# Second quantised layer of a decoder: three filling steps moved into the cross attention before it, and its first bias added by TensorE

## The reference

```
def act_quant_fake(x):
    scale = 127.0 / clip(max(abs(x), -1), 1e-05)
    return clip(round(x * scale), -128.0, 127.0) / scale
def weight_quant_fake(w):
    scale = 1.0 / clip(mean(abs(w)), 1e-05)
    return clip(round(w * scale), -1.0, 1.0) / scale
def bitlinear(x, w, b):
    return einsum('btd,hd->bth', act_quant_fake(x), weight_quant_fake(w)) + b
h = layernorm(x, ln1_g, ln1_b)           # over 128 features
h = bitlinear(h, w1, b1)                 # 128 -> 512
h = gelu(h)                              # exact
h = layernorm(h, ln2_g, ln2_b)           # over 512
h = bitlinear(h, w2, b2)                 # 512 -> 128
x = layernorm(x + h)
```

## Time and profile before

| what | us |
|---|---|
| median of 3 runs (lowest, highest) | 1842.26 (1840.89, 1844.54) |
| the profiled execution | 1842.72 |
| its span, first to last instruction | 1840.9 |
| TensorE matmuls busy | 1510.0 (82%) |
| VectorE busy | 1110.9 (60%) |
| ScalarE busy | 874.4 (47%) |
| GpSimd busy | 610.7 (33%) |
| mean granted TensorE clock, share of full speed | 0.868 |

### The profile page before, as it was taken

One profiled execution on the slowest core, in us unless ns is written; L12 is line 12 of the kernel. 1 busy time (PEld: TensorE's weight loads), 2 busy tenths in 40 slices (PEclk: granted clock), 3 DMA queues, 4 the chain that ended last, 5 costly groups with the idle time before them and its releaser, 6 DMA issues.

```text
span 1840.9 us, 44133 instructions
## 1 busy us (share of the span) xinstructions
PE 1510.0 (82%) x16485; PEld 1018.2 (55%) x16492; DVE 1110.9 (60%) x3614; ACT 874.4 (47%) x2556; POOL 610.7 (33%) x849
## 2 busy tenths in 40 slices
PE   4556369979989769898889633699799999998998
PEld 3334246646656555455557412577577777776443
DVE  3434556656757557115767688577566666664776
ACT  3222335545556335443546544344366666665443
POOL 2422232222226333001212233222244444443666
PEclk6555569989999789999999855699899999999999
DMA  6200000000000000000020000000000000000000
GB/s 239 48 1 2 1 1 3 2 1 2 2 2 2 1 0 1 1 1 2 2 119 2 24 1 0 1 3 3 24 1 1 0 0 0 0 0 1 1 12 12
DMA packets 13994, 23.96 MB, mean 13 GB/s; under 512 B 11385, under 2 KB 11769, under 8 KB 12537
## 3 DMA queue, kind: packets, MB, share of 16 engines
q1 hardware_dynamic: 13818, 21.59, 3.3%
HBM read 18.15 MB, written 1.05 MB: 10 GB/s over the span
## 4 chain that ended last, share of the span: by engine, by line
PE 66%; DVE 12%; issue 7%; ACT 6%; POOL 4%; DVEq 3%; POOLq 1%; DMA 0%; ACTq 0%; another core or an unknown queue 0%; SPq 0%
PE ps L732 5%; PE ps L653 5%; PE ps L692 5%; PE ps L2884 4%; PE ps L2533 4%; PE ps L2543 3%; PE ps L2557 3%; PE ps L2512 3%; PE ps L2519 3%; PE ps L2356 2%; PE ps L613 2%; PE ps L1315 2%; PE ps L742 2%; PE ps L2504 2%; PE ps L719 2%
## 5 line engine op out<-in xcount | busy, mean ns | idle before, releaser
L919 DVE TENSOR_REDUCE arena<-ps 128x4 f32<-128x512 f32 x320 | 204.1, 683 | 111.9 <-PE ps L653 31.4
L857 ACT ACTIVATE arena<-ps 128x512 f32<-128x512 f32 x320 | 171.7, 597 | 99.2 <-PE ps L719 96.8
L544 POOL TENSOR_TENSOR arena<-arena,C 128x512 f32<-128x512 f32 x80 | 83.1, 1040 | 392.8 <-ACT arena L878 127.5
L2449 POOL TENSOR_TENSOR arena<-arena 128x512 f32<-128x512 f32 x128 | 132.7, 1042 | 224.4 <-DVE arena L2758 223.9
L1315 PE MATMUL ps<-hid,WA 128*20 128x16 f32 x1024 | 57.0, 196 | 88.2 <-DVE hid L1368 88.2
L2676 ACT COPY arena<-ps 128x512 f32<-128x512 f32 x128 | 69.1, 588 | 123.1 <-PE ps L2543 123.1
L2667 ACT ACTIVATE arena<-ps,arena 128x256 f32<-128x256 f32 x256 | 119.9, 477 | 11.8 <-issue 8.1
L2884 PE MATMUL ps<-WA,maskadd 128*128 128x512 f32 x256 | 119.8, 598 | 1.8 <-DVE arena L3027 1.8
L732 PE MATMUL ps<-arena 128*32 128x128 f32 x2560 | 110.8, 282 | 3.2 <-ACT arena L857 3.0
L653 PE MATMUL ps<-arena 32*128 32x128 f32 x2560 | 103.9, 288 | 10.0 <-POOL arena L544 7.0
L2750 DVE TENSOR_REDUCE arena<-ps 128x2 f32<-128x512 f32 x128 | 82.4, 686 | 45.1 <-PE ps L2533 43.7
(11 more groups left out here) (455 smaller groups left out, 3834.3 us busy)
## 6 DMA issues: line engine op xcount, KB each, us to landing
WA<-w_late SPq DMA_DIRECT2D x1, 4228.0 KB, 13.7
WA<-w_early SPq DMA_DIRECT2D x1, 1600.0 KB
arena<-maskadd SPq DMA_DIRECT2D x16, 96.0 KB, 2.4
R<-rows SPq DMA_DIRECT2D x1, 1282.0 KB, 8.8
WB<-w_rest SPq DMA_DIRECT2D x1, 1152.0 KB, 11.7
x_all<-x_tok SPq DMA_DIRECT2D x1, 1024.0 KB, 15.2
arena<-mask SPq DMA_DIRECT2D x1, 1024.0 KB
ctxT_all<-ctx_T SPq DMA_DIRECT2D x1, 1024.0 KB
```

The lines of the kernel that those rows point to most:

```text
L544: nc.gpsimd.tensor_tensor(heads(v_(n % 2, ATT, "P", WIDE_Q, 512)), src.unsqueeze(1).broadcast_to([128, 4, 128]), cst("tilemask").unsqueeze ...
L857: nc.scalar.activation(v_(s, ATT, "PT", 512 * t, 512), ps[s][t][:, :], ACT.Exp, scale=SCALE).then_inc(pT_sb, 1)
L919: nc.vector.tensor_reduce(v_(z, ATT, "m", 4 * t, 4), heads(ps[z][t][:, :]), AXX, ALU.max)
L2449: nc.gpsimd.tensor_tensor(p, p, v_(z, LAT, "rec", 4 * u + 2 * x, 2).unsqueeze(2).broadcast_to([128, 2, 256]), ALU.mult).then_inc(l_sub, 1)
```

## The change

The fill of the quantised layer is issued from inside the cross attention, one layer step at the end of each of attention steps 15, 16 and 17 (`f2_early`), on all four engines; the layer's own loops then begin at step 0. For that the bodies of the four loops become functions (`ff2_pool_step`, `ff2_pe_step`, `ff2_act_step`, `ff2_dve_step`).

The first bias is no longer added by VectorE. The up product leaves u = PSUM x back; the bias is put into PSUM ahead of the scaling: VectorE multiplies the bias row once by a constant of the weights (`small[:, 10:11]`), ScalarE makes a diagonal matrix of the rows' scales, and TensorE adds diagonal x row to the up product's bank (float32, 128x128 by 512). Gelu then reads PSUM, with the scale `back`. VectorE's L2061 is gone, and its order in a step changes: output before the maxima, h's maximum ahead of n. TensorE turns n ahead of the up product.

Two further edits: in S_SELF2 the output product stands ahead of the head transposes, and the normalisation behind the cut of the maxima; and two semaphores of the mask transfers become one, so that both waits are for all 1024 counts.

```
+    if sub == S_X2 and k >= BATCH - 1:          # at the end of each satt_* step
+        ff2_pe_step(pe, f2_early(k))            # and _act_, _dve_, _pool_
+def f2_early(k):
+    return k - BATCH + 1 - F2_X

 satt_pe, end of a step
+    if sub == S_SELF2 and has(k - 1):
+        output(k - 1)
     if has(k):
         heads_T(k)
     if has(k + 2):
         front_v(k + 2)
-    if has(k - 1):
+    if sub != S_SELF2 and has(k - 1):
         output(k - 1)

 satt_dve
-    if has(k - 2):
+    if sub != S_SELF2 and has(k - 2):
         normed(k - 2)
     if has(k + 1):
         maxima(k + 1, 2, 4)
         cut_up(k + 1)
+    if sub == S_SELF2 and has(k - 2):
+        normed(k - 2)

 ff2_pe_step
     def up(n):
         pe.wait_ge(f_xnT_sb, BATCH + n + 1)
+        if n > 1:
+            pe.wait_ge(f_act, BATCH + n - 1)
+        elif n == 0:
+            pe.wait_ge(y_read, of_run(st_run[S_X2], BATCH - 1))
         nc.tensor.matmul(ps[0][n % 2][:, :], f2_(n, "hbT").bitcast(BF16), tern_up[:, :], start=True,
+                         stop=False)
+    def up_bias(n):
+        if n == 0:
+            pe.wait_ge(g_row, 1)
+        pe.wait_ge(g_diag, n + 1)
+        nc.tensor.matmul(ps[0][n % 2][:, :], f2_(n, "diag"), R[:, ROWS("ff2_up")], start=False,
                          stop=True).then_inc(f_up, 1)
+    if has(k - F2_R):
+        turned_n(k - F2_R)
+    if has(k + F2_IN):
+        up(k + F2_IN)
+    if has(k - F2_R):
+        down(k - F2_R)
+    if has(k + F2_IN):
+        up_bias(k + F2_IN)
+    if has(k + F2_H):
+        turned_h(k + F2_H)

 ff2_act_step, after the negated u and before the eviction of the turned n
+    n = k + F2_IN
+    if has(n):
+        act.wait_ge(g_scale, f2_scales(k - 1))
+        nc.scalar.activation(f2_(n, "diag"), ident, ACT.Copy,
+                             scale=f2_(k - 1, "scale", 0, 1)).then_inc(g_diag, 1)
 ff2_act_step, Gelu
-        act.wait_ge(g_in, n + 1)
-        nc.scalar.activation(f2_(n, "u"), f2_(n, "u"), ACT.Gelu).then_inc(f_act, 1)
+        act.wait_ge(f_up, BATCH + n + 1)
+        act.wait_ge(f_var, LIN_STEPS + F1_STEPS + f2_count(k - 1))
+        if n > 1:
+            act.wait_ge(g_mid, n - 1)
+        nc.scalar.activation(f2_(n, "u"), ps[0][n % 2][:, :], ACT.Gelu,
+                             scale=f2_(k - 1, "back", 0, 1)).then_inc(f_act, 1)

 ff2_dve_step
+    if k == -F2_X:
+        row = R[:, ROWS("ff2_up")]
+        nc.vector.tensor_scalar(row, row, small[:, 10:11], None, ALU.mult).then_inc(g_row, 1)
     statistics of u and x; wait for the reciprocal deviations
     h, first operation (new: waits for f_xnT of two sequences back)
-    u = PSUM x back + bias row        (128x512, scalar_tensor_tensor)
     drain; h, second operation
+    output x                          (tensor_scalar, SBUF to SBUF)
+    drain; maximum of |h|
     n; residual
     drain
-    maximum of |h|
     maximum of |n|
-    output x
     drain; unit; statistics of the residual
     drain
+    if has(k):
+        dve.wait_ge(g_diag, k + 1)
     scale by a reciprocal; back; means, variances (unchanged)

 satt_pe, entry of S_MQA
-    pe.wait_ge(g_in, BATCH)
+    pe.wait_ge(f_act, 2 * BATCH)
```

More of the change, by code:

```diff
@@ L121 @@
 FF2 = Columns(("h", 128), ("hbT", 64), ("u", FF), ("n", FF), ("nbT", FF // 2), ("xb", 128), ("r", 128), ("stats", 18),
-              ("mv", 6), ("rstd", 3), ("peak", 2), ("unit", 2), ("scale", 2), ("back", 2))
+              ("mv", 6), ("rstd", 3), ("peak", 2), ("unit", 2), ("scale", 2), ("back", 2), ("diag", 128))
 assert QKV_KEPT + FF2.size <= ARENA
@@ L841, in satt_pe @@
                     sim_turn(pe, 2, ps[0][3])
+                if sub == S_X2 and k >= BATCH - 1:
+                    ff2_pe_step(pe, f2_early(k))
         def satt_act(act, sub, kind):
@@ L899, in satt_act @@
                     sim_squared(act, 0, ps[0][2])
+                if sub == S_X2 and k >= BATCH - 1:
+                    ff2_act_step(act, f2_early(k))
         def satt_dve(dve, sub, kind):
@@ L993, in satt_dve @@
                         reg_max(k + 2)
+                if sub == S_X2 and k >= BATCH - 1:
+                    ff2_dve_step(dve, f2_early(k))
         xt_run = {S_X0: 0, S_X1: 1, S_X2: 2, S_MQA: 3, S_LAT: 4}
@@ L1975, in ff2_pe, with ff2_pool_step @@
-        def ff2_pe(pe):
+        def ff2_pool_step(pool, k):
+            if k < BATCH + F2_R:
+                taken = 1 if k < 0 else 2 if k < F2_R else 3
+                pool.wait_ge(f_var, LIN_STEPS + F1_STEPS + f2_count(k))
+                nc.gpsimd.tensor_tensor(f2_(k, "rstd", 0, taken), f2_(k, "mv", 1, 2 * taken - 1)[:, ::2],
+                                        cst("minushalf")[:, 0:taken], ALU.pow).then_inc(f_rstd, 1)
+            if has(k):
+                pool.wait_ge(g_mid, k + 1)
+                nc.gpsimd.tensor_tensor(f2_(k, "n"), f2_(k, "n"), R[:, ROWS("ff2_g2")], ALU.mult).then_inc(g_gain, 1)
+                pool.wait_ge(seq_done, ready(S_FF2, k))
+                nc.gpsimd.tensor_tensor(f2_(k, "xb"), x_all[:, k, :], R[:, ROWS("ff2_down")], ALU.add).then_inc(f_xb, 1)
@@ new lines, in ff2_act, with ff2_dve_step @@
+        def ff2_act(act):
+            for k in f2_steps()[F2_X:]:
+                ff2_act_step(act, k)
+        def ff2_dve_step(dve, k):
+            if k == -F2_X:
+                row = R[:, ROWS("ff2_up")]
+                nc.vector.tensor_scalar(row, row, small[:, 10:11], None, ALU.mult).then_inc(g_row, 1)
+            now, was = k, k - 1
+            taken = 1 if k < 0 else 2 if k < F2_R else 3
+            h, n, r, out = k + F2_H, k - F2_N, k - F2_R, k - F2_OUT
+            if has(k):
+                dve.wait_ge(f_act, BATCH + k + 1)
+                nc.vector.bn_stats(f2_(now, "stats", 6, 6), f2_(k, "u"))
+            if has(k + F2_X):
+                dve.wait_ge(seq_done, ready(S_FF2, k + F2_X))
+                nc.vector.bn_stats(f2_(now, "stats", 0, 6), x_all[:, k + F2_X, :])
+            if k > -F2_X:
+                dve.wait_ge(f_rstd, LIN_STEPS + F1_STEPS + f2_count(was))
+            if has(h):
+                if h > 1:
+                    dve.wait_ge(f_xnT, BATCH + h - 1)
+                nc.vector.scalar_tensor_tensor(f2_(h, "h"), x_all[:, h, :], f2_(was, "mv", 0, 1),
+                                               R[:, ROWS("ff2_g1")], ALU.subtract, ALU.mult)
+            if has(h):
+                dve.drain()
+                nc.vector.scalar_tensor_tensor(f2_(h, "h"), f2_(h, "h"), f2_(was, "rstd", 0, 1), R[:, ROWS("ff2_b1")],
+                                               ALU.mult, ALU.add)
+            if has(out):
+                nc.vector.tensor_scalar(x_all[:, out, :], f2_(out, "r"), f2_(was, "mv", 4, 1), f2_(was, "rstd", 2, 1),
+                                        ALU.subtract, ALU.mult).then_inc(seq_done, 1)
+            if has(h):
+                dve.drain()
+                nc.vector.tensor_reduce(f2_(now, "peak", 0, 1), f2_(h, "h"), AXX, ALU.max, apply_absolute_value=True)
+            if has(n):
+                dve.wait_ge(g_gain, n + 1)
+                nc.vector.scalar_tensor_tensor(f2_(n, "n"), f2_(n, "n"), f2_(was, "rstd", 1, 1), f2_beta[:, :],
+                                               ALU.mult, ALU.subtract)
+            if has(r):
+                dve.wait_ge(f_y, 2 * BATCH + r + 1)
+                dve.wait_ge(f_xb, 2 * BATCH + r + 1)
+                nc.vector.scalar_tensor_tensor(f2_(r, "r"), ps[1][2][:, 128 * (r % 2):128 * (r % 2) + 128],
+                                               f2_(was, "back", 1, 1), f2_(r, "xb"), ALU.mult, ALU.add)
+            dve.drain()
+            if has(n):
+                nc.vector.tensor_reduce(f2_(now, "peak", 1, 1), f2_(n, "n"), AXX, ALU.max, apply_absolute_value=True)
+            a, b = (0 if has(h) else 1), (2 if has(n) else 1)
+            if a < b:
+                dve.drain()
+                nc.vector.tensor_scalar(f2_(now, "unit", a, b - a), f2_(now, "peak", a, b - a), 1e-5, 1.0 / 127.0,
+                                        ALU.max, ALU.mult)
+            if has(r):
+                nc.vector.bn_stats(f2_(now, "stats", 12, 6), f2_(r, "r"))
+            if a < b:
+                dve.drain()
+                if has(k):
+                    dve.wait_ge(g_diag, k + 1)
+                nc.vector.reciprocal(f2_(now, "scale", a, b - a), f2_(now, "unit", a, b - a)).then_inc(g_scale, 1)
+            if a < b:
+                nc.vector.tensor_tensor(f2_(now, "back", a, b - a), f2_(now, "unit", a, b - a), small[:, 14 + a:14 + b],
+                                        ALU.mult)
+            if k >= BATCH + F2_R:
+                return
+            dve.drain()
+            for m in range(taken):
+                nc.vector.bn_aggr(f2_(now, "mv", 2 * m, 2), f2_(now, "stats", 6 * m, 6))
+            dve.drain()
+            v = f2_(now, "mv", 1, 2 * taken - 1)[:, ::2]
+            nc.vector.tensor_scalar(v, v, LN_EPS, None, ALU.add).then_inc(f_var, 1)
@@ L2105, in decoder @@
+            for k in f2_steps()[F2_X:]:
```

(1 more changed line is left out.)

156 lines of the change are left out of this document (41 added, 115 removed).

## The result

The changed kernel took 1832.45 us in the median of 7 runs (1827.55 to 1836.56), the kernel before 1840.91 beside it (1839.33 to 1844.54): ratio 0.9945, 95% interval [0.9933, 0.9957]. The profiled execution is 1832.45, its span 1830.6, against 1842.72 and 1840.9. The forecast was 1834.4 for the median. The profiled execution gains more than the median (10.3 us of span against 8.5): one more profiled execution of the same kernel, in experiment 10, gains 5.7.

The account below looks back on a forecast made before the run. VectorE, and what it waits for, was taken to set the layer's pace. Savings of 3.6+0.15+0.8+3.3+0 = 7.9 us gave 1834.8 for the profiled run and 1834.4 for the median; range 1827.0 to 1838.0.

Parts of the forecast that it names:

- Steady steps, 11 x 0.33 = 3.6: Quantised layer, steps 3 to 13: each falls from 6.69 to 6.36 us, saving 0.33, together 3.6 us.
- 0.15: Step 2 of the layer, without an output: set by the Gelu chain at 6.3 instead of 6.42, booked as 0.15 us.
- Gelu chain of 6.3: Steady step: from h's quantisation through n, down product, bias pair and Gelu to ScalarE's next quantisation, 6.3 us.
- Rival C: Steady step: VectorE's L2065 is held by GpSimd's product as well as the output; 5.3 us saved, 1836.9; 17%.
- The pair about 2.0 us and covered: Steady step, TensorE: the bias product's two float32 passes take 2.0 us, covered by VectorE's chain of 6.36.
- the ring: Steady step: Gelu, roundings, turned n, down product, bias pair, next Gelu; forecast at 6.3 us, just under VectorE's 6.36.
- Fill 3.3: Three filling steps issued inside the cross attention: the layer's full steps begin 3.3 us nearer the attention's end.
- Tail 0.8: Layer's last steps: they lose the output between maximum and unit, and L2061 once, saving 0.8 us.
- rival B: TensorE's clock rises: 11.2 us saved, 1831.1, including 2 us from multi-query attention starting warm; 13%, with or without Rival A.
- Self attention 0: Second self attention (S_SELF2): its reorder gains nothing, as VectorE waits for the same GpSimd product; upper bound 3.6 us.
- Rival A: No holding on the shared ports, and S_SELF2 gains 3.6 us: 12.4 us saved, 1829.8; 18%.
- Rival D: ScalarE: the diagonal's copy needs another function table than Gelu, two 1.28 us loads a step; 8 slower, 1850.3; 4%.

Follow-up runs that it names:

- experiment 10: Changed kernel unaltered, run again beside the kernel with the residual in PSUM and the bias pair first in the filling: 1834.15 us and 1826.1 us.
- Experiment 3: Against the changed kernel, the residual is kept in a free PSUM bank instead of SBUF: 1827.44 us, ratio 0.9941.
- experiment 6: Against the changed kernel, VectorE adds the first bias again, without diagonal and pair, and TensorE has its old order: 1837.79 us, ratio 0.9988.
- experiment 4: Against the changed kernel, the pair of TensorE passes for the first bias is left out, the diagonal still made: 1831.11 us, ratio 0.9948.
- experiment 7: Against the changed kernel, the residual is kept in PSUM and the pair for the first bias is left out: 1825.41 us, ratio 0.9923.
- experiment 2: Against the changed kernel, the filling steps go back from inside the attention to the layer's own loops: 1836.29 us, ratio 0.9979.
- experiment 1: Against the changed kernel, the reorder of the second self attention is taken back: 1829.71 us, ratio to the kernel before 0.9942.

## Why the prediction was right, step by step

- **Steady steps, 11 x 0.33 = 3.6.** Measured 6.38 against 6.36 forecast (its own terms, 4.08 and 2.3, add up to 6.38). The twelve from S(1) on gave 3.75, and the forecast's 3.6 + 0.15 is the same number partly by luck: the first of them gave 0.50 instead of 0.15 (5.92 for 6.42, so no Gelu chain of 6.3 bound it, and without the pair it is 5.93 too), and the other eleven 3.25 instead of 3.6. The output ended 0.08 after the product, and n stood at S+4.10 for the forecast S+4.08. Experiment 3 showed that this was the bound, experiment 6 that without the diagonal the step is 6.72. The output was held with its operand in SBUF (1.29 us) and not with it in PSUM (0.41), and the pass with one PSUM input was not held (0.75) beside a running product. This is the hold as described in the Trainium skill, "SBUF — State Buffer", section "SBUF: two separate sides", where the shared pair of ports is an exclusive lock for a whole instruction. Rival C (L2065, now L2110, held too) did not come: it started 0.09 ahead of the product and took 0.36; the product then took 1.39 instead of 1.27, near the 0.09 that the forecast had put on it.
- **The pair about 2.0 us and covered.** 2.02 us, ended at S+5.77 (forecast +5.55 from h's quantisation, which starts at S+0.19: S+5.74). Covered: experiment 4. "It would be the bound at 6.3" was 0.12 too long: the ring is 6.18 (experiments 3 and 7). The forecast's margin of cover was thin by its own numbers (6.3 under 6.36); it was 0.2.
- **Fill 3.3.** Measured 3.9. The second scale came 4.17 earlier, of which 0.45 are from before the stage: 3.72, as forecast (3.7). The other 0.6 is the size of one term: from that scale to S(1) the forecast took 10.6, and the changed kernel takes 10.04 (1052.56 to 1062.60). Moving the filling alone is worth 4.35 (experiment 2), because in its own loops the diagonal kernel fills 0.5 slower than the kernel before. The forecast had the pair in that loop with its whole 2.0; leaving it out gains only 1.1 (experiment 4).
- **Tail 0.8.** Work 1.2 and 0.97 in two executions; another 1.0 in the profiled one came from the clock at the next stage's start, which the forecast had only in rival B (2 us for a warm start; fully warm it was 2.4, 16.61 less 14.20).
- **Self attention 0.** 0.27, at its end (experiment 1); the steps are 5.77 in both orders, and the cast takes 0.59 instead of 0.33, as forecast.
- **Rival A** failed on the hold, **rival B** on the clock: TensorE's share rose to 66% and the granted clock stayed at 0.50 but for short rises (0.55 on average). **Rival D**: the diagonal's copy took 0.39 us with no table load in front of it. The layer has one load, 1.28 us at 1050.11, ahead of the first Gelu and hidden under the first pair (1050.27 to 1052.29).

The totals, 7.9 us forecast and 10.3 measured in the profiled execution (8.5 by medians), differ by small excesses in fill (0.6), self attention (0.3), tail (0.4) and clock (1.0). The repeat's 7.0 by medians and 5.7 in its profiled execution lie on the other side of 7.9. That the total came within 0.6 us of the median's gain is closer than such executions repeat, and so partly luck; the parts above are what bears the forecast out. The merged semaphore of the mask transfers was not run by itself.

## What to carry to other kernels

When an operation moves into another engine's shadow, ask whether it can run there: here VectorE's copy from SBUF was stretched to the end of GpSimd's product, and giving the same operation a PSUM source was worth some 0.3 us a step, at the price of a free PSUM bank. Before calling a product on another engine covered, follow the whole ring that it closes and write down its length; it is the next bound (6.18 here). And undo linked edits together: the bias alone on its old engine, with the new order elsewhere, measured a wait that neither kernel has.

## What the runs showed that I had not expected

- A VectorE operation that was already queued when it fell inside a GpSimd product waited it out whole (1.29 for 0.34), while the one before it, begun 0.09 ahead of the product, ran in 0.36 and the product grew by 0.12. The growth is a wait as well: wherever h's operation, with two SBUF inputs, began 0.08 to 0.17 ahead of the product, the product was longer (1.31 to 1.40) and ended 1.11 to 1.13 us after that operation's end, in all thirteen traces. Where it began 0.20 or more ahead, the product took its 1.26 or 1.27.
- Being ahead by a little does not spare an operation the hold: in the changed kernel's step at 1068.52 the output began 0.07 ahead of the product (1071.05, 1071.12) and was held all the same, for 1.42 us. That step took 6.51.
- The changed kernel has one step of 6.73 instead of 6.38, and so has each variant that leaves VectorE's order and operands as they are (its repeat and experiments 1, 2 and 4). In the changed kernel VectorE stood idle after the output for nothing that the profile shows, 0.35 longer than the usual 0.09:

```profile
1122.21 1.28 DVE L2113 TENSOR_SCALAR x_all<-arena 128x128 f32<-128x128 f32 x1
1123.94 0.28 DVE L2117 TENSOR_REDUCE arena<-arena 128x1 f32<-128x128 f32 x1 [0.44 <-issue]
```

  With the residual in PSUM the same 0.44 stood at 1116.73, and the wait for GpSimd's product hid it. The kernel before has its long step too (7.03 in place of 6.69), with 0.42 of the same kind ahead of its maximum of h. What causes it is open.
- The granted clock stayed at the lower level with TensorE busy 66% of 67 us in steps with gaps, apart from short rises; in experiment 3 one of them made one pair 1.76 us instead of 2.02 (1081.05) and one round from Gelu to Gelu 5.92 instead of 6.18.
